# One fused kernel on Trainium2: the first down-projection pieces made inside the last gate/up products, the residual added by TensorE, and the last output tile finished in halves

## What is computed

```python
gate = h @ (gate_w + gate_b @ gate_a).T      # 2752 hidden columns, 1024 features, rank 16
up   = h @ (up_w + up_b @ up_a).T
y    = x3 + (silu(gate) * up) @ (down_w + down_b @ down_a).T
```

## Time and profile before

| | |
|---|---|
| time, median of 3 runs | 1338.87 us (1337.48 to 1339.25) |
| the profiled execution's own time | 1337.44 us |
| its span, first to last instruction | 1335.3 us |
| TensorE busy | 1232.9 us (92%) |
| VectorE / ScalarE / GpSimd busy | 622.5 / 398.7 / 42.0 us |
| mean granted TensorE clock | 0.962 of full speed |

### The profile page before, as it was taken

How to read it: one execution, slowest core, us unless ns; L and a number is a source line. 1 busy time by engine, 2 the same in 40 slices (tenths; PEclk the granted TensorE clock), 3 DMA queues, 4 the chain that set the end, 5 groups by cost and what they waited for, 6 DMA issues and landing times.

```text
span 1335.3 us, 15541 instructions
## 1 busy us (share of the span) xinstructions
PE 1232.9 (92%) x6557; PEld 608.9 (46%) x6562; DVE 622.5 (47%) x1057; ACT 398.7 (30%) x526; POOL 42.0 (3%) x50
## 2 busy tenths in 40 slices
PE   3899999268899999899999999999999969999998
PEld 2435565143444444454444444444444434444443
DVE  7694999879375435544333333333321152222220
ACT  7774242675325332322112121211111111111110
POOL 4400000000010000000000000000000000000000
PEclk9887999778999999999999999999999979999999
DMA  9520000011015321102111111112100031121120
GB/s 376 193 89 33 1 1 1 0 48 38 17 56 171 126 78 50 32 17 63 48 48 48 48 48 48 51 45 63 36 25 6 0 92 55 43 59 43 53 96 32
DMA packets 24901, 79.32 MB, mean 59 GB/s; under 512 B 3520, under 2 KB 4160, under 8 KB 24832
## 3 DMA queue, kind: packets, MB, share of 16 engines
q1 hardware_dynamic: 24832, 78.33, 17.9%
HBM read 74.12 MB, written 4.19 MB: 59 GB/s over the span
## 4 chain that ended last, share of the span: by engine, by line
PE 86%; DVE 8%; ACT 4%; issue 2%; DMA 0%; DVEq 0%; SPq 0%; ACTq 0%
PE PAIR L1504 25%; PE PAIR L1506 25%; PE PAIR L1505 24%; PE PAIR L1569 2%; PE PAIR L1586 2%; DVE X L1078 2%; PE PAIR L1784 1%; PE PAIR L1601 1%; DVE X L1084 1%; PE PAIR L1667 1%; PE PAIR L1577 1%; PE PAIR L1817 1%; ACT POOL L443 1%; DVE BST L944 1%; DVE LORA L1156 1%
## 5 line engine op out<-in xcount | busy, mean ns | idle before, releaser
L1504 PE MATMUL PAIR<-XT,POOL 128*128 128x512 f16 (+1 forms) x832 | 316.4, 380 | 8.5 <-DVE POOL L1109 5.9
L1505 PE MATMUL PAIR<-XT,POOL 128*128 128x512 f16 (+1 forms) x832 | 316.3, 380 | 0.0
L1506 PE MATMUL PAIR<-XT,POOL 128*128 128x512 f16 (+1 forms) x832 | 316.2, 380 | 0.0
L1504 PE MATMUL PAIR<-POOL 128*128 128x512 f16 x704 | 270.2, 384 | 6.7 <-DVE POOL L1109 6.7
L1506 PE MATMUL PAIR<-POOL 128*128 128x512 f16 x704 | 269.8, 383 | 0.0
L1505 PE MATMUL PAIR<-POOL 128*128 128x512 f16 x704 | 269.6, 383 | 0.0
L1504 PEld LDWEIGHTS PAIR<-XT,POOL 128*128 128x128 f16 (+1 forms) x832 | 81.9, 98 | 102.8 <-DVE POOL L1109 6.5
L1506 PEld LDWEIGHTS PAIR<-XT,POOL 128*128 128x128 f16 (+1 forms) x832 | 81.9, 98 | 98.5 <-issue 1.1
L1505 PEld LDWEIGHTS PAIR<-XT,POOL 128*128 128x128 f16 (+1 forms) x832 | 82.0, 99 | 92.9 <-issue 1.1
L1504 PEld LDWEIGHTS PAIR<-POOL 128*128 128x128 f16 x704 | 69.4, 99 | 89.4 <-DVE POOL L1109 7.6
L1181 DVE SCALAR_TENSOR_TENSOR PAIR<-PAIR,POOL 128x1024 f32<-128x1024 f32 (+1 forms) x22 | 27.1, 1232 | 173.9 <-PE PAIR L1506 173.9
(11 more groups left out here) (218 smaller groups left out, 1220.6 us busy)
## 6 DMA issues: line engine op xcount, KB each, us to landing
STG<-in_gate_w SPq DMA_DIRECT2D x21, 512.0 KB, 3.5
STG<-in_up_w SPq DMA_DIRECT2D x21, 512.0 KB, 3.5
STG<-in_ctx_t SPq DMA_DIRECT2D x16, 512.0 KB, 3.6
STG<-in_ctx SPq DMA_DIRECT2D x16, 512.0 KB, 4.1
STG<-in_down_w SPq DMA_DIRECT2D x16, 512.0 KB, 3.5
POOL<-in_ctx SPq DMA_DIRECT2D x12, 512.0 KB, 11.1
X<-in_x SPq DMA_DIRECT2D x8, 512.0 KB, 9.6
out_t<-XT SPq DMA_DIRECT2D x16, 256.0 KB, 2.9
```

The source lines that it names most:

```text
L1504: e.matmul(dst, l_hi, r_hi, start=first, stop=False)
L1505: e.matmul(dst, l_hi, r_lo, start=False, stop=False)
L1506: return e.matmul(dst, l_lo, r_hi, start=False, stop=last)
```

## The change

- `DB` and `DA` are copied from staging at n = 40 of VectorE's loop over the products, in place of after it.
- Tile 0's folds go into TensorE's stream: two pieces ahead of gate product 42, the third between its two halves, the fourth ahead of up product 43. VectorE adds and makes the low halves after `hidden(20)`, ScalarE makes the high halves ahead of the silu of product 42. Tile 1's additions start right behind `hidden(21)`.
- The float32 transposes of `X`, their copies and the residual addition on VectorE go. In their place `X` is split into two f16 parts `XR` (ScalarE and VectorE, 8 instructions each, after the last up product, between the pieces of tile 1), and after the steps of a tile 16 matmuls of 128 columns add both parts in PSUM. Their weights are blocks of `XR`, their moving operand is a scaled identity `IDR`.
- A finished tile is scaled out of PSUM in two halves, the first by ScalarE, the second by VectorE, into `X`, from where it is sent.
- Tile 7 does all steps of sequence 0 first and then those of sequence 1. The other tiles keep their order.
- POOL makes one more constant at the start, and the scratch space for dynamic transfers is set to 1024 bytes.

The diff, without the declarations of semaphores:

```diff
+        IDR = sb("IDR", [P, P], F16)
...
-        XT3 = XT[:, :, :, :, :].rearrange("p b s k t -> p (b s k t)").bitcast(F32)\
-            .rearrange("p (m t) -> p m t", m=KD)
+        XR = XT[:, :, :, :, :].rearrange("p b s k t -> p (b s k t)").rearrange("p (g s d) -> p g s d", g=NT, s=2)
...
-            + [(("down", m), out_v, 2 * m + 2) for m in range(KD)]))
+            + [(("down", m), None, 0) for m in range(KD)]))
...
-            + [(("r", 0), xt3_ok, 1)]
-            + [(("dfold", 0, i), d_add, i + 1) for i in range(NP)]
-            + [u for m in range(1, KD) for u in
-               [(("dfold", m, i), d_add, m * NP + i + 1) for i in range(NP)] + [(("r", m), xt3_ok, m + 1)]]))
+            + [(("dfold", m, i), d_add, m * NP + i + 1) for m in range(KD) for i in range(NP)]))
...
             for m in range(KD):
-                for h in range(2):
+                for h, done in enumerate((out_a, out_v)):
                     hs = slice(h * HALF, (h + 1) * HALF)
-                    e.wait_ge(out_v, 2 * m + h + 1)
-                    e.dma_start(out_t[m * P:(m + 1) * P, hs], XT3[:, m, hs]).then_inc(out_done, 16)
+                    e.wait_ge(done, m + 1)
+                    e.dma_start(out_t[m * P:(m + 1) * P, hs], X[:, m, hs]).then_inc(out_done, 16)
...
-            for n, (dst, fill) in enumerate(((NEG1, -1.0), (NEGM, -WS * WS))):
+            for n, (dst, fill) in enumerate(((NEG1, -1.0), (NEGM, -WS * WS), (IDR, HS * WS))):
...
-                    e.wait_ge(down_p, m - 1)
+                    e.wait_ge(down_p, 2 * (m - 1))
                 e.activation(DWN[(m + 1) % 2][0:kp, 0, k0:k1, :], st, ACT.Copy).then_inc(d_hi, 1)
-            def residual(m):
-                e.wait_ge(r_p, m + 1)
+            def residual_hi(g):
+                e.wait_ge(x3_ok, g + 1)
                 e.wait_ge(gu_p, 2 * HT)
-                e.activation(XT3[:, m, :], PAIR[aux.pair("r", m)][:, :], ACT.Copy).then_inc(xt3_ok, 1)
+                e.activation(XR[:, g, 0, :], X[:, g, :], ACT.Copy).then_inc(xr_hi, 1)
+
+            def finish(m):
+
+                e.wait_ge(down_p, 2 * m + 1)
+                e.wait_ge(xr_lo, NT)
+                e.activation(X[:, m, 0:HALF], PAIR[main.pair("down", m)][:, 0:HALF], ACT.Copy,
+                             scale=1.0 / (HS * WS)).then_inc(out_a, 1)
...
             for n in range(2 * HT):
                 if fill_between(n) < 2 * HT:
                     slab_hi(fill_between(n))
+                if n == 2 * HT - 2:
+                    for i in range(NP):
+                        down_hi(0, i)
                 if n % 2:
                     hidden_hi(n // 2)
                 else:
                     silu(n // 2)
-            residual(0)
             for i in range(NP):
-                down_hi(0, i)
+                residual_hi(2 * i)
+                residual_hi(2 * i + 1)
+                down_hi(1, i)
             for m in range(KD):
-                if m:
-                    residual(m)
-                if m + 1 < KD:
+                if 0 < m < KD - 1:
                     for i in range(NP):
                         down_hi(m + 1, i)
+                finish(m)
...
+            def residual_lo(g):
+                e.wait_ge(xr_hi, g + 1)
+                e.tensor_tensor(XR[:, g, 1, :], X[:, g, :], XR[:, g, 0, :], ALU.subtract).then_inc(xr_lo, 1)
+
             def finish(m):
-                e.wait_ge(down_p, m + 1)
-                e.wait_ge(xt3_ok, m + 1)
-                for h in range(2):
-                    hs = slice(h * HALF, (h + 1) * HALF)
-                    e.scalar_tensor_tensor(XT3[:, m, hs], PAIR[main.pair("down", m)][:, hs], 1.0 / (HS * WS),
-                                           XT3[:, m, hs], ALU.mult, ALU.add).then_inc(out_v, 1)
+
+                e.wait_ge(down_p, 2 * m + 2)
+                e.wait_ge(xr_lo, NT)
+                e.tensor_scalar(X[:, m, HALF:D], PAIR[main.pair("down", m)][:, HALF:D], 1.0 / (HS * WS), None,
+                                ALU.mult).then_inc(out_v, 1)
...
+                elif f == 2 * HT + 1:
+                    factor(N_DF, DB, 2, WS)
+                    factor(N_DF + 1, DA, 1, 1.0)
                 if n % 2:
                     hidden(n // 2)
-            factor(N_DF, DB, 2, WS)
-            factor(N_DF + 1, DA, 1, 1.0)
+                if n == 2 * HT - 3:
+                    for i in range(NP):
+                        down_add(0, i)
+                        down_lo(0, i)
             for i in range(NP):
-                down_add(0, i)
-                down_lo(0, i)
+                residual_lo(2 * i)
+                residual_lo(2 * i + 1)
+                down_add(1, i)
+                down_lo(1, i)
             for m in range(KD):
-                if m + 1 < KD:
+                if 0 < m < KD - 1:
...
-            def residual_transpose(m):
-                pr = aux.pair("r", m)
-                aux.wait_empty(e, "r", m)
-                for g in range(NT):
-                    i = e.transpose(PAIR[pr][:, g * P:(g + 1) * P], X[:, g, m * P:(m + 1) * P], IDF[:, :])
-                i.then_inc(r_p, 1)
-
             def down_fold(m, i):
                 k0, k1 = PIECES[i]
                 pr = aux.pair("dfold", m, i)
                                     DB[0:GRP * 32, m * P:(m + 1) * P], start=True, stop=True)
                 last.then_inc(dfold_p, 1)
-            def down(m, k):
+            def down(m, b, k):
                 pr, dw = main.pair("down", m), DWN[(m + 1) % 2]
                 if k == 0:
-                    main.wait_empty(e, "down", m)
+                    if m < 2:
+                        main.wait_empty(e, "down", m)
+                    else:
+                        e.wait_ge(out_v if b else out_a, m - 1)
                 kp = P if k < HT - 1 else HTAIL
-                e.wait_ge(d_lo, m * NP + (min(k // 8, 2) if k < HT - 1 else 3) + 1)
+                if b == 0:
+                    e.wait_ge(d_lo, m * NP + (min(k // 8, 2) if k < HT - 1 else 3) + 1)
                 if m == 0:
                     e.wait_ge(hid_lo, k + 1)
-                for b in range(B):
-                    bs = slice(b * S, (b + 1) * S)
-                    i = mm3(PAIR[pr][:, b * HALF:(b + 1) * HALF], dw[0:kp, 0, k, :], dw[0:kp, 1, k, :],
-                            HIDT[0:kp, k, 0, bs], HIDT[0:kp, k, 1, bs], k == 0, k == HT - 1)
-                if k == HT - 1:
-                    i.then_inc(down_p, 1)
+                bs = slice(b * S, (b + 1) * S)
+                mm3(PAIR[pr][:, b * HALF:(b + 1) * HALF], dw[0:kp, 0, k, :], dw[0:kp, 1, k, :],
+                    HIDT[0:kp, k, 0, bs], HIDT[0:kp, k, 1, bs], k == 0, k == HT - 1)
+
+            def residual(m, b):
+
+                pr = main.pair("down", m)
+                if m == 0:
+                    e.wait_ge(xr_lo, b * BT + BT)
+                for t in range(BT):
+                    ts = slice(b * HALF + t * P, b * HALF + (t + 1) * P)
+                    for j in range(2):
+                        i = e.matmul(PAIR[pr][:, ts], XR[:, b * BT + t, j, m * P:(m + 1) * P], IDR[:, :], start=False,
+                                     stop=True, skip_group_check=True)
+                i.then_inc(down_p, 1)
...
+                if n == 2 * HT - 2:
+                    down_fold(0, 0)
+                    down_fold(0, 1)
+                elif n == 2 * HT - 1:
+                    down_fold(0, 3)
                 if n >= 2:
                     gate_up(n, 0)
+                if n == 2 * HT - 2:
+                    down_fold(0, 2)
                 gate_up(n, 1)
             for m in range(KD):
-                residual_transpose(m)
-                if m == 0:
-                    for i in range(NP):
-                        down_fold(0, i)
-                for k in range(HT):
-                    down(m, k)
-                    if m + 1 < KD and k % 5 == 2 and k // 5 < NP:
-                        down_fold(m + 1, k // 5)
+                if m < KD - 1:
+                    for k in range(HT):
+                        for b in range(B):
+                            down(m, b, k)
+                        if k % 5 == 2 and k // 5 < NP:
+                            down_fold(m + 1, k // 5)
+                    for b in range(B):
+                        residual(m, b)
+                else:
+                    for b in range(B):
+                        for k in range(HT):
+                            down(m, b, k)
+                        residual(m, b)
...
-    nc = bacc.Bacc("TRN2", target_bir_lowering=False, num_devices=1)
+    nc = bacc.Bacc("TRN2", target_bir_lowering=False, num_devices=1, dynamic_dma_scratch_size=1024)
```

More of the change, by code:

```diff
@@ L204, in build @@
             sem(n) for n in ("ctk_ok", "pt_lo", "c_lo", "max_ok", "rsum_ok", "at_lo", "x3_ok", "x4t_lo", "x3v_lo"))
-        fac_ok, s_add, s_lo, hid_v, hid_lo, d_add, d_lo, out_v = (
-            sem(n) for n in ("fac_ok", "s_add", "s_lo", "hid_v", "hid_lo", "d_add", "d_lo", "out_v"))
```

(6 more changed lines are left out.)

## The result

The changed kernel takes 1319.88 us (median of 4 runs, 1317.51 to 1321.08) against 1338.96 us (4 runs, 1337.48 to 1339.25). The ratio is 0.9858, with a 95% interval of 0.984 to 0.9875. That is 19.1 us less, where 17.95 and a time of 1320.9 were forecast. The profiled execution has 1320.61 us, with a span of 1318.8.

A forecast was written before the change was run, and what follows sets the result against it. TensorE, busy 92% of the span, was taken as the bound, with a removable stand-still before the down product. 16.27 + 1.96 - 0.77 - 0.11 + 0.60 = 17.95 us off 1338.87 gave 1320.9 us; range 1318.5 to 1325.

The forecast's parts named there:

- The early pieces: Between last up product and first down matmul: tile 0's inputs ready by product 43's end, 17.72 - 1.45 = 16.27 us gained.
- The room at each step: Slack before TensorE asks for tile 0's inputs: 9 us for the factors, least 1.2 us at the first addition.
- The clock: Tile 0 of the down product: full clock without the stand-still ahead, 33.04 - 31.08 = 1.96 us gained.
- The residual on TensorE: Behind each tile: 16 f16 matmuls at 0.057 us replace eight float32 transposes, costing 0.77 us.
- Both slow prices: Residual matmuls: 0.079 us each if weight loads bind (10%), 0.22 if each waits for its predecessor (2% full, 2% half).
- the rival that would have made the kernel slower: Residual matmuls: second part waits for the first, 20.9 us more, 1341.8; chance 2%, plus 2% for half, 1331.3.
- Tile 7: Last tile by sequences: three more weight-shape changes, 0.27 us, less 0.16 for shorter last-matmul latency, costing 0.11 us.
- The tail: Behind the last matmul: one VectorE instruction of 512 columns in place of two, 0.60 us gained, up to 0.95.
- The lower bound of the term: Last VectorE scaling: at least about half of 0.69 us, since a 96x1024 scaling out of staging took 0.68.

The follow-up runs named there:

- the filled gap: Kernel before, with 68 thrown-away matmuls of 512 columns in TensorE's stand-still behind product 43; median 1335.88 us, ratio 0.9983.
- the run with late pieces: Changed kernel with tile 0's factors, folds, additions and halves moved back behind product 43, rest kept; median 1338.14 us, ratio 0.9997.
- the doubled residual: Changed kernel with every residual matmul issued twice, 32 for a tile; median 1327.40 us.

## Why the prediction was right

The last stretch fell from 291.35 to 273.50, by 17.85 us, where the sum said 17.95. The mechanism was the predicted one, and the small miss is in tile 7. By its terms:

- *The early pieces*: 16.27 forecast, 16.26 measured. The room at each step came out as followed. The run with the factors one product later shows what carries it. The run with early pieces alone shows that 15.3 of it need nothing else of the change; the other 0.9 are tile 0's transposes, which only count once the wait is gone.
- *The clock*: 1.96 forecast. Tile 0 fell from 33.04 to 31.07, and the filled gap shows that the stand-still is the cause, not VectorE's work beside the tile. The size is that of one execution: behind the same waits the run with late pieces lost 1.43 in tile 0 (32.49 - 31.06), and the one with late factors had five slow large matmuls. The term came out to 0.01 because forecast and result are both set against the same execution of the kernel before; it is no measure of the price in others.
- *The residual on TensorE*: 0.77 forecast. A set costs 0.90, where 0.91 was forecast, and a boundary 1.21, where it was 1.23, so 8 x 0.90 - 7 x 0.93 = 0.69. Both slow prices, and with them the rival that would have made the kernel slower, fell by the doubled residual.
- *Tile 7*: mis-sized. From its first matmul to VectorE's start it grew from 28.79 to 30.00, by 1.21, of which 0.90 is the residual, so 0.31 for the order where 0.11 was summed. The three changes of shape are there (0.31 between starts and not 0.22), and so is the shorter latency: from the last matmul's start to VectorE's start it was 0.41 and is 0.26. What the sum left out is that the last large matmul, which used to end the stream, now takes its own distance of 0.22 before the next, while the last residual matmul's 0.06 isn't spent. 0.27 + 0.22 - 0.06 - 0.15 = 0.28.
- *The tail*: 0.60 forecast. From the last matmul's end to the span's end it is 1318.8 - 1315.30 = 3.50, and was 4.19, so 0.69. The new instruction takes 0.69, as its neighbour did, which gives the 0.60. The rest is behind VectorE's end: 2.8 with one last transfer, 2.9 before with two. That it is because no other transfer runs beside the last one is not shown. The lower bound of the term leaned on one row of 0.68 for a 96x1024 scaling out of staging; another of the same instruction took 1.25, so that row bounded nothing.

The median is 1.0 us under the forecast and the profiled execution 1.1 over the 1319.5 that its own sum gave. For the profiled one this is what lies ahead of product 41, where it was 1.35 us later than that of before, and where the change leaves TensorE's stream as it was. For the median it can't be told from the spread of several us, so that it came within 1.0 is no finer proof than the last stretch.

## What to carry to other kernels

When a stage begins with a chain over several engines, look for the last point at which each engine is free before it and put each link there, starting from the one that everything waits for: here the factor copies on VectorE, 7.9 us in all, decided 13.5 of 17.9 us by their place. Swapping one operation for another of equal cost, as the residual here, moves little, however much of the diff it is (with the halved end, 0.56 us gained once the wait was gone, and 0.4 lost where it stood). And a stand-still on TensorE costs more than its length, so where it can't be removed, matmuls into a bank that is overwritten next give a part back.

## What the runs showed that was not expected

- Executions of one program differ by up to 8 us (1335.06 to 1343.06 in 19 runs of the kernel before). Some of it sits in the clock behind short waits, how much is not shown. The wait of 3.34 us ahead of score 4 was followed by full clock in the profiled executions of before and after. In that of the kernel with late pieces, with the same wait, the lower one followed:

```profile
345.00:365.00 20.00, 16.71 (x78) 0.91 0.03 7
443.00:463.00 20.00, 16.66 (x70) 0.91 0.35 105
556.00:582.00 26.00, 22.59 (x108) 0.87 0.07 24
```

  The stretch from 443 on has 0.91 in place of 1.00, and eight matmuls of 512 columns 0.43 apart. What decides it is not shown. The same holds for how long it lasts: nine slow large matmuls behind the long wait before, seven with late pieces.
- Matmuls of 128 columns with a weight load each run 0.056 apart in runs of 32, though four in succession add into the same columns.
